# Moving the value copies and the second logits group at the head of a window-attention step

## The chip, the cores and the metric

One core of a Trainium2 chip runs the whole kernel. The metric is device time in microseconds (us) of one execution, lower is better.

## The reference

A Swin block on an input of 32 images of 56 x 56 tokens with 128 channels: layer norm, a cyclic shift by 3, windows of 7 x 7 tokens, attention with 16 heads of 8 channels with a relative position bias and a mask for the shifted edge windows, projection, residual; then layer norm, an MLP 128 to 512 to 128 with GELU, residual.

```python
y = _ln(x, norm1_g, norm1_b)
y = jnp.roll(y, (-SS, -SS), axis=(1, 2))
yw = y.reshape(B, nWh, WS, nWw, WS, C).transpose(0, 1, 3, 2, 4, 5).reshape(B * nW, N, C)
qkv = yw @ qkv_w.T + qkv_b
...
attn = jnp.einsum('bhqd,bhkd->bhqk', q * scale, k)
...
attn = jax.nn.softmax(attn.reshape(B * nW, HEADS, N, N), axis=-1)
o = jnp.einsum('bhqk,bhkd->bhqd', attn, v)
...
o = o @ proj_w.T + proj_b
...
x = shortcut + o
h = _ln(x, norm2_g, norm2_b)
h = jax.nn.gelu(h @ fc1_w.T + fc1_b, approximate=False)
h = h @ fc2_w.T + fc2_b
return x + h
```

## The kernel before

The work is cut into 128 steps: 8 bands of 7 rows by 16 pairs of images. A step holds two images side by side (partitions 0 to 48 and 64 to 112 of most tiles) and 8 windows of each. The steps run as a software pipeline written out by hand: body `t` of each engine holds, in a fixed order, pieces of step `t+3` (load and statistics) down to step `t-3` (store). Each engine runs its own program in order, and waits on counting semaphores; nothing reorders at run time. So the order of the calls in each body is the order on the engine.

What matters here is the head of a body and its window loop, `for w in range(NW)` with `NW = 8`. A turn of that loop handles one window of both images (the change's title calls it a pair):

- TensorE (PE) makes the values of step `t` (line 910, 24 matmuls): windows 0 to 3 into PSUM bank 7 (`s_v` counts one), windows 4 to 7 into bank 6 (`s_v` counts two). Then it projects the attention output of step `t-1` (line 919, 14 matmuls in two signalled halves, 4 and 3 rows). Then comes the loop: `logits(t, w)` (lines 780 and 785, into banks 2 to 5, two window buffers), `pv(t, u)` (line 800, probabilities times values, into bank 6) in the even turns from 2, `fc2` of step `t-2` (lines 832 and 837, into bank 7) in the odd turns, and `max_logits(t+1, w)` (line 750, into banks 0 and 1), the logits of the next step, of which only the row maxima are needed.
- `max_logits(t+1, 0)` waits until the operands `mx_k` and `mx_q` are in (`s_mx_dma`; SyncE, whose queue is SPq, issues them at lines 273 and 277), and until VectorE (DVE) has read the projection out of banks 0 and 1 (`s_x1`, line 682). `max_logits(t+1, w)` for a later `w` waits for the row maxima of `w-1` (`s_max`).
- VectorE casts the hidden layer (`hid_high`, line 580), copies one quarter of the values (line 673, image 0 of bank 7) to `v_own`, adds projection and residual (`x1`, line 682, two halves), and then, in the loop, takes the row maxima (`row_maxima`, line 587) with pieces of layer norm statistics (line 506) in between.
- ScalarE (ACT) does two GELUs (line 421), loads the table of exp (`load_table`, line 397: a table load and a one-element activation), copies two quarters of the values (line 483, image 1 of both banks), then `exp` of window 0 (line 406), the last quarter of the values (line 488, image 0 of bank 6), and the other `exp`s, with copies of `pv` (line 414).
- GpSimd (POOL) makes `hid_lo` (line 375) from the GELU output, which the last matmuls of `fc2` (line 837) need.

`v_place(im, b)` is the place of one image and one bank in `v_own`, `v_made(im, b)` the PSUM it is copied from (bank `7 - b`). `logits(t, w)` waits for `exp` of `w-2` where it reuses a buffer, and `pv(t, 0)` for `exp` of windows 0 and 1 and for all value copies. `fc2(t-2, 1, ...)` in turn 1 writes bank 7, and so waits until the values in it have been copied.

Of the kernel before, what the change touches and what calls it, by code (L numbers as in the profile page):

```python
# [9 lines left out]
ACT = mybir.ActivationFunctionType  # L10
# [39 lines left out]
def swin_block_kernel(nc, x, wqT, wkT, wvT, wvpT, wpT, w1T, w2T, cols, rows, table_k, table_q, ident, eye,  # L50
# [11 lines left out]
    with ctx:  # L62
# [324 lines left out]
        @block.scalar  # L387
        def _(act):
            act.wait_ge(s_w, 16 * N_W)

            nc.scalar.mul(w_q, w_q, HD ** -0.5).then_inc(s_inita, 1)
            nc.scalar.mul(col[:, BQ:BQ + 1], col[:, BQ:BQ + 1], HD ** -0.5).then_inc(s_inita, 1)
            act.wait_ge(s_inita, 2)

            def load_table(function):

                nc.scalar.activation(scrap[:, :], col[0:1, 0:1], function)

            def exp_pair(n, w):
                if w >= 4 or past(n, 0):  # L400
                    act.wait_ge(s_pv, NU * n + w // 2 - 1)
                act.wait_ge(s_st, NW * n + w + 1)
                if w < CH and exists(n - 2):
                    act.wait_ge(s_hid_lo, CH * (n - 2) + w + 1)
                b = 2 + 2 * (w % 2)
                nc.scalar.activation(probs[0:KP, w % 4, :].rearrange("p (b c) -> p b c", b=2),  # L406
                                     ps[0:KP, b:b + 2, 0:HB * WT], ACT.Exp).then_inc(s_exp, 1)

            def copy_pv(n, u):
                act.wait_ge(s_pv, NU * n + u + 1)  # L410
                if u == 0 and past(n, 0):
                    act.wait_ge(s_o_dma, N_O * n)
                    act.wait_ge(s_sum_dma, N_SUM * n)
                nc.scalar.activation(pv_sb[:, :, 2 * u * WT:2 * (u + 1) * WT],  # L414
                                     ps[:, 6, 0:NG * 2 * WT].rearrange("p (g q) -> p g q", g=NG),
                                     ACT.Copy).then_inc(s_pv_sb, 1)

            def gelu(n, c):
                act.wait_ge(s_fc1, CH * n + c + 1)
                bank = 2 + 2 * (c % 2)  # L420
                nc.scalar.activation(hid[:, c, :].rearrange("p (b q) -> p b q", b=2), ps[:, bank:bank + 2, 0:HT],  # L421
                                     ACT.Gelu, bias=col[:, BF + c:BF + c + 1], scale=1 / W_SCALE).then_inc(s_gelu, 1)

            def body(t, edge, odd):
                if exists(t - 1):
                    copy_pv(t - 1, NU - 1)
                n = t - 2
                if exists(n):
                    act.wait_ge(s_t2, n + 1)
                    if past(n, 0):  # L430
                        act.wait_ge(s_fc1, CH * n)
                    nc.scalar.activation(h_hi[:, :].rearrange("p (i c) -> p i c", c=TP),
                                         tokens_of(2)[:, 0:WS, 0:TP], ACT.Copy).then_inc(s_h_hi, 1)
                n = t + 1
                if exists(n):

                    act.wait_ge(s_t1, n + 1)
                    if past(n, 1):
                        act.wait_ge(s_v, 2 * (n - 1))
                    else:  # L440
                        act.wait_ge(s_initp, 1)
                    src = tokens_of(0)[:, 0:WS, 0:TP].rearrange("p i (m c) -> p i m c", m=2)
                    dst = yT_hi[odd(1)][:, :, :, 0:WT].rearrange("p w m (i j) -> p w m i j", i=WS)
                    last_w = NW - 1
                    kept = WS - SS
                    def put(o, a):
                        return nc.scalar.activation(o, a, ACT.Copy)
                    for im in range(2):
                        put(dst[:, 0:last_w, im, :, :].rearrange("p w i j -> p i w j"),
                            src[:, :, im, SS:SS + last_w * WS].rearrange("p i (w j) -> p i w j", j=WS))  # L450
                    put(dst[:, last_w, :, :, 0:kept].rearrange("p m i j -> p i m j"),
                        src[:, :, :, W - kept:W])
                    put(dst[:, last_w, :, :, kept:WS].rearrange("p m i j -> p i m j"),
                        src[:, :, :, 0:SS]).then_inc(s_y_hi, 1)
                if exists(t - 2):
                    load_table(ACT.Gelu)
                    gelu(t - 2, 0)
                    gelu(t - 2, 1)
                n = t + 1
                if exists(n):  # L460

                    if past(n, 0):
                        act.wait_ge(s_mx_dma, N_MX * n)
                        act.wait_ge(s_st_dma, N_ST * n)
                    for j, (hi, bank, b) in enumerate(((k_hi, 0, BK), (q_hi, 6, BQ))):
                        act.wait_ge(s_qk, 2 * n + j + 1)
                        nc.scalar.activation(hi[:, :, :, :].rearrange("p w m q -> p m w q"),
                                             ps[:, bank:bank + 2, 0:BT].rearrange("p m (w q) -> p m w q", w=NW),
                                             ACT.Identity, bias=col[:, b:b + 1]).then_inc(s_hi, 1)
                if exists(t - 2):  # L470
                    gelu(t - 2, 2)
                    gelu(t - 2, 3)
                if exists(t):
                    load_table(ACT.Exp)
                n = t
                if exists(n):
                    if past(n, 0):
                        act.wait_ge(s_pv, NU * n)
                    else:
                        act.wait_ge(s_init, 2)  # L480
                    for b in range(2):
                        act.wait_ge(s_v, 2 * n + b + 1)
                        nc.scalar.activation(v_place(1, b), v_made(1, b), ACT.Copy).then_inc(s_vown_b, 1)
                if exists(t):
                    for w in range(NW):
                        exp_pair(t, w)
                        if w == 0:
                            nc.scalar.activation(v_place(0, 1), v_made(0, 1), ACT.Copy).then_inc(s_vown_b, 1)
                        if w % 2 == 0 and w > 0:
                            copy_pv(t, w // 2 - 1)  # L490

            turns(body)


        @block.vector
        def _(dve):
# [96 lines left out]
            def body(t, edge, odd):  # L593
# [70 lines left out]
                if exists(t - 2):  # L664
                    hid_high(t - 2, 2)
                    hid_high(t - 2, 3)
                n = t
                if exists(n):

                    if past(n, 0):  # L670
                        dve.wait_ge(s_pv, NU * n)
                    dve.wait_ge(s_v, 2 * n + 1)
                    nc.vector.tensor_copy(v_place(0, 0), v_made(0, 0)).then_inc(s_vown, 1)
                n = t - 1
                if exists(n):

# [8 lines left out]
                for w in range(NW):  # L685
                    if exists(t + 1):
                        row_maxima(t + 1, w)
                    n = t - 1
                    if exists(n):

                        if w in (0, 1):
                            stats(x1, st2, (2 * w, 2 * w + 2))
                        if w == 2:
                            stats(x1, st2, (4, WS)).then_inc(s_st2, 1)
                        if w == 3:
                            aggregate(n, st2, s_st2, mv2, s_ln2)
                    n = t + 3
                    if exists(n):

                        if w == 4:  # L700
                            dve.wait_ge(s_x, loads(n, edge(n)))
                            stats(x_in[odd(3)], st1, (0, 1))
                        if w == 5:
                            stats(x_in[odd(3)], st1, (1, 4))
                        if w == 6:
                            stats(x_in[odd(3)], st1, (4, WS)).then_inc(s_st1, 1)
# [8 lines left out]
        def _(pe):  # L715
# [102 lines left out]
            def fc2(n, p, i):  # L818
                first, end = FC2_PARTS[p]
                if i == first and p == 1:  # L820
                    pe.wait_ge(s_hid_hi, CH * (n + 1))
                    if exists(n + 2):
                        pe.wait_ge(s_vown, n + 3)
                        pe.wait_ge(s_vown_b, 3 * (n + 2) + 1)
                    elif n > 0:
                        pe.wait_ge(s_fin, 2 * n)
                if i == first and p == 0:
# [13 lines left out]
            def body(t, edge, odd):  # L841
# [78 lines left out]
                        last.then_inc(s_proj, 1)  # L920
                for w in range(NW):
                    if exists(t):
                        if w != 1:
                            logits(t, w, edge, odd(0))
                        if w == 0:
                            logits(t, 1, edge, odd(0))
                        if w % 2 == 0 and w > 0:
                            pv(t, w // 2 - 1)
                    if exists(t - 2) and w % 2:
# [67 lines left out]
```

## Time and profile before

| | |
|---|---|
| median of three runs | 3900.76 us (3899.22 to 3903.62) |
| the profiled execution | 3904.86 us, its span 3903.1 us |
| busy share of the span | PE 96%, DVE 79%, POOL 74%, ACT 71% |
| granted TensorE clock, mean | 0.993 of full speed |

The span runs from the first to the last instruction in the trace; what lies around it is 1.8 us. Times in the trace are from the start of the span. A matmul's record begins at its issue and ends with a modelled end, so records of neighbouring matmuls overlap.

### The profile page before, as it was taken

The numbers are of one execution on the slowest core, as the hardware profiler recorded it, in microseconds if no ns is written. First come the engines' busy times: TensorE is split into PE (matmuls) and PEld (weight loads), VectorE is DVE, ScalarE is ACT, GpSimd is POOL, SyncE is SP. The second block draws the span as 40 slices with busy tenths as digits, with TensorE's granted clock in tenths as the row PEclk, the third lists the DMA queues.
The fourth block names the chain that finished last, engine by engine and source line by source line (L and its number), as shares of the span: only waits on it lengthen the run. The fifth ranks groups of instructions, "written<-read, shape, count | busy, mean of one in ns | idle before, by whom it ended". The sixth has DMA issues, their size and how long they took to land. (4 is left out here: it accounts for less than half of the span.)

```text
span 3903.1 us, 176619 instructions
## 1 busy us (share of the span) xinstructions
PE 3744.1 (96%) x75664; PEld 2946.8 (76%) x75664; DVE 3087.1 (79%) x7840; ACT 2776.0 (71%) x3840; POOL 2884.4 (74%) x3988
## 2 busy tenths in 40 slices
PE   2899999999999999999999999999999999999997
PEld 1677777777777777777777777777777777777776
DVE  6788878878878878878887888888888788888874
ACT  1677777777777777777777777777777777777774
POOL 5577777777777777777777777777777777777775
PEclk8999999999999999999999999999999999999999
DMA  2343334434434434433433344333344334333331
GB/s 76 106 119 118 115 112 118 119 111 116 121 114 115 118 115 118 117 115 115 118 117 111 115 119 116 114 117 116 111 118 120 112 116 119 115 115 117 117 108 58
DMA packets 603457, 441.97 MB, mean 113 GB/s; under 512 B 135939, under 2 KB 602227, under 8 KB 602675
## 3 DMA queue, kind: packets, MB, share of 16 engines
q1 hardware_dynamic: 602211, 428.86, 37.2%
q8 instruction: 597, 9.78, 1.1%
q14 instruction: 185, 1.52, 0.1%
q0 software_dynamic: 464, 1.81, 0.1%
HBM read 106.14 MB, written 51.46 MB: 40 GB/s over the span
## 5 line engine op out<-in xcount | busy, mean ns | idle before, releaser
L587 DVE TENSOR_REDUCE neg_max<-ps 113x16 f32<-113x784 f32 x1024 | 999.6, 976 | 545.5 <-PE ps L750 439.1
L406 ACT ACTIVATE probs<-ps 113x784 f32<-113x784 f32 x1024 | 848.1, 828 | 656.9 <-PE ps L785 539.5
L375 POOL TENSOR_TENSOR hid_lo<-probs,hid_hi 128x784 f16<-128x784 f32 x512 | 881.3, 1743 | 76.6 <-DVE hid_hi L580 76.3
L785 PE MATMUL ps<-st_q,st_k 128*49 128x196 f16 x8192 | 694.5, 249 | 0.0
L780 PE MATMUL ps<-bias,eye_k 106*64 106x392 f16 x4096 | 684.3, 331 | 0.0
L750 PE MATMUL ps<-mx_k,mx_q 128*49 128x196 f16 x8192 | 541.6, 253 | 60.3 <-DVE neg_max L587 52.4
L785 PEld LDWEIGHTS ps<-st_q,st_k 128*49 128x49 f16 x8192 | 440.2, 105 | 125.4 <-issue 0.5
L421 ACT ACTIVATE probs<-ps,col 128x784 f32<-128x784 f32 x512 | 467.6, 913 | 89.5 <-PE ps L814 60.1
L832 PE MATMUL ps<-w_hi,hid_hi 128*112 128x128 f16 x3584 | 521.7, 226 | 3.8 <-DVE hid_hi L580 3.0
L832 PE MATMUL ps<-w_lo,hid_hi 128*112 128x128 f16 x3584 | 498.8, 220 | 0.0
L832 PEld LDWEIGHTS ps<-w_hi,hid_hi 128*112 128x112 f16 x3584 | 417.7, 130 | 83.8 <-issue 79.4
L800 PE MATMUL ps<-probs,v_own 113*32 113x49 f32 x32768 | 470.3, 209 | 8.3 <-issue 7.6
L800 PEld LDWEIGHTS ps<-probs,v_own 113*32 113x32 f32 x32768 | 397.1, 110 | 92.3 <-issue 90.9
L750 PEld LDWEIGHTS ps<-mx_k,mx_q 128*49 128x49 f16 x8192 | 317.3, 103 | 137.6 <-DVE neg_max L587 74.4
L832 PEld LDWEIGHTS ps<-w_lo,hid_hi 128*112 128x112 f16 x3584 | 419.1, 131 | 0.0
L338 POOL TENSOR_SCALAR x_in<-x_in,rs,nm 112x128 f32<-112x128 f32 x896 | 389.4, 450 | 13.5 <-POOL nm L333 0.4
L338 POOL TENSOR_SCALAR z<-x,rs,nm 112x128 f32<-112x128 f32 x896 | 388.7, 450 | 13.5 <-POOL nm L333 0.4
L329 POOL TENSOR_TENSOR rs<-ve,half 112x7 f32<-112x7 f32 x256 | 380.4, 1486 | 21.3
L414 ACT ACTIVATE pv_sb<-ps 128x392 f32<-128x392 f32 x512 | 255.2, 498 | 182.0 <-PE ps L800 171.4
L356 POOL TENSOR_SCALAR r_hi<-sums 128x98 f16<-128x98 f32 x128 | 36.4, 284 | 461.3 <-DVE sums L628 461.3
L350 POOL TENSOR_TENSOR x_res<-x_res,proj_b 112x896 f32<-112x896 f32 x128 | 268.9, 2101 | 131.2 <-DMA x_res<-in_x 131.1
L837 PE MATMUL ps<-w_hi,hid_lo 128*112 128x128 f16 x3584 | 349.3, 220 | 3.4 <-POOL hid_lo L375 3.4
(119 smaller groups left out, 8009.9 us busy)
## 6 DMA issues: line engine op xcount, KB each, us to landing
st_k<-k_hi SPq DMA_DIRECT2D x256, 196.0 KB
st_q<-q_hi SPq DMA_DIRECT2D x1024, 49.0 KB
oT_raw<-pv_sb SPq DMA_DIRECT2D x256, 196.0 KB, 3.8
x_in<-in_x SPq DMA_DIRECT2D x224, 196.0 KB
x_res<-in_x SPq DMA_DIRECT2D x224, 196.0 KB
out_y<-y_out SPq DMA_DIRECT2D x224, 196.0 KB
mx_k<-k_hi SPq DMA_DIRECT2D x512, 49.0 KB
mx_q<-q_hi SPq DMA_DIRECT2D x128, 196.0 KB
```

Source lines behind the costliest of these rows:

```text
L329: nc.gpsimd.tensor_tensor(rs[:, :], ve[:, :], half[:, :], ALU.pow).then_inc(s_rs, 1)
L338: last = nc.gpsimd.tensor_scalar(z[:, i, :], src[:, i, :], rs[:, i:i + 1], nm[:, i:i + 1], ALU.mult, ALU.add)
L375: nc.gpsimd.tensor_tensor(hid_lo[:, c, :], hid[:, c, :], hid_hi[:, c, :], ALU.subtract).then_inc(s_hid_lo, 1)
L406: nc.scalar.activation(probs[0:KP, w % 4, :].rearrange("p (b c) -> p b c", b=2), ps[0:KP, b:b + 2, 0:HB * WT], ACT.Exp).then_inc(s_exp, 1)
L421: nc.scalar.activation(hid[:, c, :].rearrange("p (b q) -> p b q", b=2), ps[:, bank:bank + 2, 0:HT], ACT.Gelu, bias=col[:, BF + c:BF + c + ...
L587: nc.vector.tensor_reduce(neg_max[0:KP, :, :, w].rearrange("p e g -> p g e"), ps[0:KP, 0:2, :].rearrange("p b (g c) -> p (b g) c", g=2)[:, ...
L750: last = mm(group(im, 0, g, 256), mx_q[edge(n)][:, g, span], mx_k[:, g, :, span], start=True, stop=True)
L780: mm(ps[HP * im:HP * (im + 1), bank + b, 0:HB * WT], eye_k[0:BIAS_ROWS, kind, im, :], bias[0:BIAS_ROWS, b, :], start=True, stop=False)
L785: last = mm(group(im, bank, g, EQ * WT), st_k[par][:, g, span], st_q[par][:, :, g, span], start=False, stop=(g % 2 == 1))
L800: last = mm(ps[32 * r:32 * r + VC, 6, first:first + WT], v_own[0:KP, w, h, :], probs[0:KP, w % 4, h * WT:(h + 1) * WT], start=True, stop=True)
L832: mm(row, hid_hi[:, c, i * TP:(i + 1) * TP], w_part[:, c, :], start=(c == 0 and w_part is w2_hi), stop=False)
L837: last = mm(row, hid_lo[:, c, i * TP:(i + 1) * TP], w2_hi[:, c, :], start=False, stop=(c == CH - 1))
```

## The change

Three edits. ScalarE copies both images of bank 7 as soon as the values of windows 0 to 3 are there, ahead of its table load, and image 0 of bank 6 after the first `exp`, as before. VectorE no longer copies image 0 of bank 7 ahead of `x1`; it copies image 1 of bank 6 after the row maxima of turn 0. On TensorE the logits of window 1 come in turn 1, behind `max_logits(t+1, 0)`, and no longer ahead of it; the wait of `fc2` for bank 7 is changed to match.

```diff
@@ ScalarE body @@
-                if exists(t):
-                    load_table(ACT.Exp)
                 n = t
                 if exists(n):
                     if past(n, 0):
                         act.wait_ge(s_pv, NU * n)
                     else:
                         act.wait_ge(s_init, 2)
-                    for b in range(2):
-                        act.wait_ge(s_v, 2 * n + b + 1)
-                        nc.scalar.activation(v_place(1, b), v_made(1, b), ACT.Copy).then_inc(s_vown_b, 1)
+                    act.wait_ge(s_v, 2 * n + 1)
+                    for im in range(2):
+                        nc.scalar.activation(v_place(im, 0), v_made(im, 0), ACT.Copy).then_inc(s_vown_b, 1)
+                    load_table(ACT.Exp)
                 if exists(t):
                     for w in range(NW):
                         exp_pair(t, w)
                         if w == 0:
+                            act.wait_ge(s_v, 2 * t + 2)
                             nc.scalar.activation(v_place(0, 1), v_made(0, 1), ACT.Copy).then_inc(s_vown_b, 1)
@@ VectorE body @@
-                n = t
-                if exists(n):
-
-                    if past(n, 0):
-                        dve.wait_ge(s_pv, NU * n)
-                    dve.wait_ge(s_v, 2 * n + 1)
-                    nc.vector.tensor_copy(v_place(0, 0), v_made(0, 0)).then_inc(s_vown, 1)
@@
                     if exists(t + 1):
                         row_maxima(t + 1, w)
+                    if w == 0 and exists(t):
+                        if past(t, 0):
+                            dve.wait_ge(s_pv, NU * t)
+                        dve.wait_ge(s_v, 2 * t + 2)
+                        nc.vector.tensor_copy(v_place(1, 1), v_made(1, 1)).then_inc(s_vown, 1)
@@ TensorE fc2 @@
                     if exists(n + 2):
-                        pe.wait_ge(s_vown, n + 3)
-                        pe.wait_ge(s_vown_b, 3 * (n + 2) + 1)
+                        pe.wait_ge(s_vown_b, 3 * (n + 2) + 2)
@@ TensorE body @@
                     if exists(t):
-                        if w != 1:
-                            logits(t, w, edge, odd(0))
-                        if w == 0:
-                            logits(t, 1, edge, odd(0))
+                        logits(t, w, edge, odd(0))
```

## Rows read from the trace of the kernel before

**Rows 1.** The page's busy times; then one step's length, busy times and granted clock.

```profile
PE 3744.1 (96%) x75664; PEld 2946.8 (76%) x75664; DVE 3087.1 (79%) x7840; ACT 2776.0 (71%) x3840; POOL 2884.4 (74%) x3988
...
1948.37:1977.62 29.25, 28.92 (x595) 22.85 (x592) 23.66 (x62) 21.70 (x31) 21.55 (x31) 1.00 0.41 117
```

**Rows 2.** Waits of TensorE: engine line waited for: us, times, longest.

```profile
PE ps L750 <- DVE neg_max L587: 52.4, 140, 1.1
...
PE ps L750 <- DMA mx_q<-q_hi: 4.4, 1, 4.4
```

**Rows 3.** TensorE's timeline, head of one step: start, us, what [idle before].

```profile
1947.60 0.22 PE L910 MATMUL ps<-wv_lo,yT_hi 128*128 128x128 f16 x1
...
1948.36 1.78 PE L919 MATMUL ps<-w_p,oT 128*112 128x128 f32 x14
1950.07 0.36 PE L780 MATMUL ps<-bias,eye_k 106*64 106x392 f16 x2
...
1950.78 0.33 PE L780 MATMUL ps<-bias,eye_k 106*64 106x392 f16 x2
...
1951.46 0.51 PE L750 MATMUL ps<-mx_k,mx_q 128*49 128x196 f16 x8
1951.90 0.26 PE L832 MATMUL ps<-w_hi,hid_hi 128*112 128x128 f16 x1
...
1953.11 0.53 PE L750 MATMUL ps<-mx_k,mx_q 128*49 128x196 f16 x8 [0.33 <-DVE neg_max L587]
1953.47 0.33 PE L780 MATMUL ps<-bias,eye_k 106*64 106x392 f16 x2
...
1954.25 0.90 PE L800 MATMUL ps<-probs,v_own 113*32 113x49 f32 x64
1955.08 0.53 PE L750 MATMUL ps<-mx_k,mx_q 128*49 128x196 f16 x8
...
1956.22 0.26 PE L832 MATMUL ps<-w_hi,hid_hi 128*112 128x128 f16 x1
...
1957.03 0.44 PE L750 MATMUL ps<-mx_k,mx_q 128*49 128x196 f16 x6
```

**Rows 4.** VectorE's timeline over the same head.

```profile
1948.22 1.04 DVE L580 CAST hid_hi<-probs 128x784 f16<-128x784 f32 x2
1949.17 1.08 DVE L673 COPY v_own<-ps 49x512 f32<-49x512 f32 x1
1950.09 1.14 DVE L682 TENSOR_TENSOR x<-ps,x_res 112x512 f32<-112x512 f32 x2
1952.07 0.98 DVE L587 TENSOR_REDUCE neg_max<-ps 113x16 f32<-113x784 f32 x1 [0.85 <-DVE x L682]
1952.97 0.47 DVE L506 BATCH_NORM_STATS2 st<-x 112x6 f32<-112x128 f32 x2
1953.68 0.98 DVE L587 TENSOR_REDUCE neg_max<-ps 113x16 f32<-113x784 f32 x1 [0.24 <-PE ps L750]
```

**Rows 5.** Second half of x1, from the groups by shape: busy us, mean ns.

```profile
L682 DVE TENSOR_TENSOR x<-ps,x_res 112x384 f32<-112x384 f32 x128 | 68.6, 536 | 0.5 <-PE ps L919 0.5
```

**Rows 6.** GpSimd's timeline over the same head.

```profile
1948.86 3.57 POOL L375 TENSOR_TENSOR hid_lo<-probs,hid_hi 128x784 f16<-128x784 f32 x2 [0.56 <-DVE hid_hi L580]
```

**Rows 7.** ScalarE's timeline over the same head.

```profile
1945.66 1.91 ACT L421 ACTIVATE probs<-ps,col 128x784 f32<-128x784 f32 x2
1947.58 1.28 ACT L397 ACT_TABLE_LOAD   x1
1948.88 0.20 ACT L397 ACTIVATE scrap<-col 1x1 f32<-1x1 f32 x1
1949.09 2.08 ACT L483 ACTIVATE v_own<-ps 49x512 f32<-49x512 f32 x2
1951.19 0.82 ACT L406 ACTIVATE probs<-ps 113x784 f32<-113x784 f32 x1
1951.91 1.06 ACT L488 ACTIVATE v_own<-ps 49x512 f32<-49x512 f32 x1
1952.78 0.85 ACT L406 ACTIVATE probs<-ps 113x784 f32<-113x784 f32 x1
```

**Rows 8.** SyncE's queue, head of the same step, then of the step at 947 us.

```profile
1947.80 0.60 SPq L277 DMA_DIRECT2D mx_q<-q_hi  x1
1948.45 1.12 SPq L186 DMA_DIRECT2D out_y<-y_out  x2
...
946.63 0.60 SPq L277 DMA_DIRECT2D mx_q<-q_hi  x1
947.27 2.08 SPq L186 DMA_DIRECT2D out_y<-y_out  x2
```

**Rows 9.** DMA issues: KB each, median us from issue to landing.

```profile
oT_raw<-pv_sb SPq DMA_DIRECT2D x256, 196.0 KB, 3.8
...
r_rows<-r_lo SPq DMA_DIRECT2D x128, 24.5 KB, 2.4
```

## The prediction

> **What bounds the kernel now.** I read the busy shares first: TensorE is busy 96% of the span and no other engine over 79% [rows 1]. In a middle step it is busy 28.92 of 29.25 us at a granted clock of 1.00 [rows 1], which is its upper level, 2.4 GHz. So only what removes an idle stretch of TensorE, or adds one, can move the time. The view of waits says which idle stretch recurs in every step: line 750, the row-maximum logits, waits for VectorE's row maxima, 52.4 us in 140 waits, about one a step of 128 [rows 2]. TensorE's timeline gives the place: the second `max_logits` of the loop, at 1953.11, after 0.33 us idle [rows 3]. An `fc2` block followed by `max_logits` without a wait takes 1957.03 - 1956.22 = 0.81 us, here it takes 1953.11 - 1951.90 = 1.21, so the stall is **0.40 us** [rows 3]. Its cause is a chain: x1 ends at 1950.09 + 1.14 = 1951.23 [rows 4]; `max_logits` 0 is issued at 1951.46, when the logits of window 1 are out of the way [rows 3]; its row maxima run 1952.07 to 1953.05 [rows 4], and TensorE goes on 0.06 later. I take 0.06 us for every signal below. All working is for this step; the other steps without DMA trouble should look alike.
>
> **The change, part by part.** The times are what each event would become.
>
> *VectorE's copy leaves the way of x1.* It costs 1.08 us there [rows 4]. x1 then waits for TensorE: the first half needs 8 of the 14 projection matmuls, which are issued 1950.07 - 1948.36 over 14 = 0.12 us apart, so it can start at about 1949.55, after the cast (1949.26). The second half needs all 14, which end at 1948.36 + 1.78 = 1950.14 [rows 3], and takes 0.54 [rows 5]. x1 ends at 1950.20 + 0.54 = 1950.74, which is 0.49 earlier.
>
> *`max_logits` 0 ahead of logits 1.* Logits 0 are out at 1950.78 [rows 3], x1's signal comes at 1950.80, so `max_logits` 0 starts at **1950.80**, 0.66 earlier. The row maxima of window 0 follow at the same distance: 1951.41 to 1952.39. TensorE meanwhile: `max_logits` takes 1953.47 - 1953.11 = 0.36, logits with the change to `fc2` or `pv` 1954.25 - 1953.47 = 0.78 [rows 3]. So `fc2` starts at 1951.94 (now 1951.90), and `max_logits` 1 at 1952.75, 0.36 earlier. The maxima (1952.45 with the signal) no longer hold it. Nothing was added to TensorE: 0.36 is almost the whole stall. `fc2`'s last matmuls need `hid_lo`, which GpSimd ends at 1948.86 + 3.57 = 1952.43 [rows 6]; the last of the 12 is issued about 0.7 after the first, at 1952.6. It is covered, by 0.1 us. The new condition of `fc2` for bank 7 is covered by far (below, 1949.97). Unheld, TensorE would go on to logits 2 at 1953.11, `pv` 0 at 1953.89 and `max_logits` 2 at 1953.89 + 0.83 = 1954.72.
>
> *ScalarE.* Its wait for the values moves ahead of the table load. Bank 7 is written when 12 of 24 matmuls are through: 1947.60 + 0.22 = 1947.82 [rows 3]. The GELUs end at 1947.57 [rows 7], so ScalarE idles 0.3 us, which it did not before; queued behind are the table load and all `exp`s. Copies: 1947.88, and 2.08 for two to 1949.96. The table load with its one-element activation takes 1949.09 - 1947.58 = 1.51 [rows 7], so `exp` 0 starts at **1951.48** instead of 1951.19. From the start of `exp` 0 to the end of `exp` 1, with the copy in between, 1953.63 - 1951.19 = 2.44 [rows 7]: `exp` 1 ends at 1953.92, and `pv` 0 can start at **1953.98**. That holds TensorE by 0.09 us. Against 1954.25 the gain left is **0.27 us**.
>
> *VectorE's copy, now inside the loop.* Row maxima 0 end at 1952.39; copy (1.08), two statistics (0.47) and row maxima 1 (0.98) follow, each starting 0.09 before the one ahead ends, as now [rows 4]: 1952.39 + 1.08 + 0.47 + 0.98 - 0.27 = 1954.65, signal at 1954.71. `max_logits` 2 would be issued at 1953.98 + 0.83 = 1954.81, now 1955.08. So it is hidden, with 0.1 us to spare, and the step still keeps 0.27. `pv` 0 needs this copy at 1953.98; it ends at 1953.38. From there the loop has slack: the 140 waits on line 587 are about one a step [rows 2], so the later turns do not hold TensorE.
>
> *The table load beside the Trainium skill.* At this place the row shows 1.28 us of load begun 0.01 after the GELU's end, and the next activation 0.02 behind the load [rows 7]: no drain is to be seen. The Trainium skill (ScalarE: Activation LUTs, What ACT_TABLE_LOAD costs) gives 1283 ns for the load, which agrees, and a drain of about 1380 ns on each switch, which these rows do not show; by it, `pv` 0 would come 1.4 us later and the step would be slower by 1.1, a rival below.
>
> *The operands' transfer.* `max_logits` 0 is now wanted 0.66 earlier, and `mx_q` is the last of its five transfers, issued at 1947.80 [rows 8]. No row has its landing. Bounds: 2.4 us, a small transfer of the same queue, gives 1950.2; from above, TensorE had to wait for it only once in the kernel's 128 steps [rows 2], so it lands by about 1951.4, 3.6 us after issue (`oT_raw`, of its size, takes 3.8 [rows 9]). The first costs nothing; the second holds `max_logits` 0, and with it logits 1, `exp` 1 and the maxima, by 0.6 us, and takes all of the gain. I take the low end for most steps, since 2.4 is also the latency of the nearest single transfer, and a wait of 0.2 us for one step in five: the queue is sometimes slow (the same two issues of `out_y` behind it took 2.08 us instead of 1.12 [rows 8]). That is 0.04 us a step.
>
> *The rest.* What lies behind the loop, the chains of the sums and of `r_rows` to the next head among them, starts from the last `pv` of the step and moves with it. Semaphore conditions and the order of the first and last steps cost or give nothing that can be seen.
>
> **Sum.** 0.27 - 0.04 = 0.23 us a step; some 126 steps have both neighbours: 29 us. Against the profiled execution 3904.86 - 29 = 3876; the median of the runs is 4 us lower, 3900.76 - 29 = **3872 us**.
>
> **Rivals.**
> 1. *The exp chain does not hold.* If ScalarE's chain is 0.1 shorter than worked out, TensorE keeps 0.36: 126 x 0.36 = 45 us, 3856. For it: the margins are of 0.1 us. Against it: every term is a row. Chance 0.1.
> 2. *A transfer takes the stall's place.* `mx_q` lands near the upper bound in most steps; the stall moves from row maxima to the DMA and the time stays at 3895 to 3902. For it: `oT_raw`'s 3.8 us [rows 9]. Against it: those go two at a time, `mx_q` alone. Chance 0.08; a half-way case (0.1 to 0.15 left, 3882 to 3890) 0.12.
> 3. *The loop's copy binds VectorE.* Were the copy or the statistics 0.4 us longer in turn 0, `max_logits` 2 would wait as long as `max_logits` 1 did: 3898. Against it: the same shape took 1.08 in its old place. Chance 0.03.
> 4. *Slower: the table load behind the copies.* The load now lies on the chain from the values to `exp` 1 and `pv` 0. The chain decides from 0.27 us more than I worked out. If the switch cost twice there what it costs now, the 1.28 of a second load [rows 7], `pv` 0 comes at 1955.26, 1.0 us later than now: 126 us, 4027. This is the size of what the Trainium skill (ScalarE: Activation LUTs, What ACT_TABLE_LOAD costs) would add as a drain. Against it: the load shows no gap on either side [rows 7], and it is the same load after a like activation. A smaller lengthening (0.1 beyond the bound) gives 3913. Chance 0.05.
>
> **How the numbers follow.** The forecast, 3862 to 3881, has 0.62, rival 1 has 0.10, rival 2 0.20 with its half-way case, rival 3 0.03, rival 4 0.05. The range runs from 3858, just short of rival 1's end, to 3890, the half-way case's end; outside are most of rivals 1 to 4 proper, under 0.2. A change of 0.2% (8 us) is about what a measurement can tell from none. Faster by more than that: forecast, rival 1, half-way, a little of the rest, 0.86; same 0.09; slower 0.05.
>
> **What would show each step.** In the profile after: x1 beginning about 0.3 after the cast and ending 0.6 after the last projection matmul; `max_logits` 0 some 2.4 us after the first projection matmul (now 3.1); the 52.4 us of line 750 on line 587 nearly gone; line 800 with a new wait of about 0.1 us a step for `exp`; `exp` 0 about 0.3 later against the projection. Line 750 waiting for `mx_q` in many steps would show rival 2, a gap at the table load rival 4, line 750 still on line 587 in turn 2 rival 3. The prediction is wrong if the pitch of the steps, 29.25 us in this one, does not fall by 0.2 to 0.3.

## The result, and the profile after

The changed kernel takes 3918.31 us (median of 4 runs, 3915.66 to 3925.03), the kernel before 3901.45 beside it: ratio 1.0047, 95% interval 1.0034 to 1.0060. It is slower, by 17 us; the prediction was 3872. The profiled execution has a span of 3916.8 us at a mean granted clock of 0.994.

With the same work and nearly the same clock, TensorE is busy 27 us more than before and VectorE 49 us more (3744.1 and 3087.1 [rows 1]); how the waits of TensorE changed tells more. The page's first part, then the view of waits (engine, line, waited for: us in total, times, longest), TensorE's matmuls (PE) first and then its weight loads (PEld), which wait ahead of the matmuls. Lines 748 and 798 are lines 750 and 800 of the kernel before.

```profile
PE 3770.8 (96%) x75664; PEld 2948.0 (75%) x75664; DVE 3135.8 (80%) x7840; ACT 2800.4 (71%) x3840; POOL 2894.2 (74%) x3988
...
PE ps L748 <- DVE neg_max L587: 15.0, 31, 1.1
...
PEld ps L748 <- DVE neg_max L587: 48.8, 139, 1.4
PEld ps L798 <- ACT probs L406: 40.2, 122, 0.6
...
PEld ps L748 <- issue: 20.3, 103, 0.6
PEld ps L748 <- DMA mx_q<-q_hi: 12.0, 24, 5.0
```

The matmuls' own wait for row maxima fell from 52.4 to 15.0 us [rows 2], and this could be read as the forecast gain. It is not: the weight loads still wait for them once a step (139 times), if for less time than in the kernel before:

```profile
PEld ps L750 <- DVE neg_max L587: 74.4, 140, 1.4
```

They also wait once a step for `exp` (122 times, against 4 before). A wait can stand at the weight load and not at the matmul behind it, so one must read both rows.

TensorE's timeline gives the places, in a step whose projection begins at 1869.92 (before: 1948.36):

```profile
1869.92 1.78 PE L916 MATMUL ps<-w_p,oT 128*112 128x128 f32 x14
...
1872.49 0.53 PE L748 MATMUL ps<-mx_k,mx_q 128*49 128x196 f16 x8
1872.83 0.35 PE L778 MATMUL ps<-bias,eye_k 106*64 106x392 f16 x2
...
1874.44 0.53 PE L748 MATMUL ps<-mx_k,mx_q 128*49 128x196 f16 x8
...
1875.77 0.90 PE L798 MATMUL ps<-probs,v_own 113*32 113x49 f32 x64
1876.79 0.53 PE L748 MATMUL ps<-mx_k,mx_q 128*49 128x196 f16 x8
```

Counted from the start of the projection, as all times are from here on:

| issued at | before [rows 3] | worked out | after |
|---|---|---|---|
| `max_logits` 0 | 3.10 | 2.44 | 2.57 |
| `max_logits` 1 | 4.75 | 4.39 | 4.52 |
| `pv` 0 | 5.89 | 5.62 | 5.85 |
| `max_logits` 2 | 6.72 | 6.45 | 6.87 |

The step is ahead at `max_logits` 1, hardly so at `pv` 0, and behind at `max_logits` 2. `pv` 0 takes 0.83 us in the kernel before (5.89 to 6.72), and here 1.02 pass. The rest is `max_logits` 2 waiting for VectorE. Its timeline, in the same step:

```profile
1869.79 1.04 DVE L580 CAST hid_hi<-probs 128x784 f16<-128x784 f32 x2
1871.19 1.16 DVE L675 TENSOR_TENSOR x<-ps,x_res 112x512 f32<-112x512 f32 x2 [0.36 <-PE ps L916]
1873.11 0.98 DVE L587 TENSOR_REDUCE neg_max<-ps 113x16 f32<-113x784 f32 x1 [0.77 <-DVE x L675]
1874.12 1.10 DVE L685 COPY v_own<-ps 49x512 f32<-49x512 f32 x1
1875.26 0.49 DVE L506 BATCH_NORM_STATS2 st<-x 112x6 f32<-112x128 f32 x2
1875.76 0.97 DVE L587 TENSOR_REDUCE neg_max<-ps 113x16 f32<-113x784 f32 x1
```

From row maxima 0 to the end of row maxima 1, VectorE works through its queue with gaps of 0.01 to 0.04 us: 3.62 us (1873.11 to 1876.73), end at 6.81, `max_logits` 2 at 6.87. Before it was 2.59 with a pause of 0.24 [rows 4]. ScalarE, same step:

```profile
1869.49 2.25 ACT L481 ACTIVATE v_own<-ps 49x512 f32<-49x512 f32 x2 [0.35 <-PE ps L907]
1871.75 1.28 ACT L397 ACT_TABLE_LOAD   x1
1873.05 0.20 ACT L397 ACTIVATE scrap<-col 1x1 f32<-1x1 f32 x1
1873.26 0.82 ACT L406 ACTIVATE probs<-ps 113x784 f32<-113x784 f32 x1
1873.98 1.08 ACT L488 ACTIVATE v_own<-ps 49x512 f32<-49x512 f32 x1
1874.86 0.86 ACT L406 ACTIVATE probs<-ps 113x784 f32<-113x784 f32 x1
```

The two copies take 2.25 us instead of 2.08 [rows 7]; `exp` 0 starts at 3.34, `exp` 1 ends at 5.80.

Over 118 steps of the two traces, the mean issue of `max_logits` 2 went from 6.78 to 6.91, and the mean step from 29.51 to 29.64: 0.13 us in some 126 steps is 16 us, nearly the whole difference of 17.

### The profile page after: what moved, and what is told of

Its sections match the earlier page's. It is cut to its first block, busy times and chain, and to the rows that moved or that the text cites. A ratio compares the mean times of both kernels' runs of the same rounds, so it can differ in the third digit from the quotient of the medians.

```text
span 3916.8 us, 176619 instructions
## 1 busy us (share of the span) xinstructions
PE 3770.8 (96%) x75664; PEld 2948.0 (75%) x75664; DVE 3135.8 (80%) x7840; ACT 2800.4 (71%) x3840; POOL 2894.2 (74%) x3988
## 4 chain that ended last, share of the span: by engine, by line
PE 40%; DVE 5%; issue 3%; DMA 1%; POOL 1%; SPq 1%; ACT 0%; POOLq 0%; DVEq 0%; ACTq 0%
PE ps L812 6%; PE ps L829 5%; PE ps L748 5%; PE ps L798 5%; PE ps L778 4%; PE ps L783 3%; PE ps L879 3%; PE ps L916 3%; PE ps L834 2%; PE ps L907 2%; DVE v_own L685 2%; DVE neg_max L587 2%; PE ps L850 1%; PE ps L858 1%; DMA r_rows<-r_lo 1%
## 5 line engine op out<-in xcount | busy, mean ns | idle before, releaser
L783 PEld LDWEIGHTS ps<-st_q,st_k 128*49 128x49 f16 x8192 | 448.4, 105 | 121.1 <-issue 0.3
```

What stands on the lines that cost most here:

```text
L783: last = mm(group(im, bank, g, EQ * WT), st_k[par][:, g, span], st_q[par][:, :, g, span], start=False, stop=(g % 2 == 1))
```

## The experiments

The theory, called A in the expectations: VectorE's queue in turn 0 of the loop (row maxima 0, the copy, two statistics, row maxima 1) has become the bound of each step; behind it, ScalarE's chain (copies, table load, `exp` 0, copy, `exp` 1) holds `pv` 0 by less. Turn 0 is the first turn of the loop. The first rival is that the order of TensorE does the harm (B in the expectations), others that the order alone would bring the gain and the copies spoil it (C), that the copy harms in another way, or the table load. Names in the diffs are as in the change.

**Each half alone.** `order_only` is the kernel before with the change of TensorE's order and nothing else:

```diff
-                        if w != 1:
-                            logits(t, w, edge, odd(0))
-                        if w == 0:
-                            logits(t, 1, edge, odd(0))
+                        logits(t, w, edge, odd(0))
```

> Theory A (VectorE's turn 0 binds, and every part of the change needs the others): x1 still ends 2.87 us after the first projection matmul, so max_logits 0 can be issued at about 3.0 instead of 3.11, but logits 1 (0.68) now lie behind it: max_logits 1 at 4.95 instead of 4.75, slower by 0.2 us a step, about 3926. Rival B (the new order of TensorE is what costs the 17 us, the copies are neutral): 3918. Rival C (the order alone brings the gain that was forecast, the copies spoil it): 3870 to 3890.

3924.24 us beside 3900.2, ratio 1.0060 (1.0043 to 1.0077). `copies_only` is the changed kernel with these four lines put back:

```diff
-                        logits(t, w, edge, odd(0))
+                        if w != 1:
+                            logits(t, w, edge, odd(0))
+                        if w == 0:
+                            logits(t, 1, edge, odd(0))
```

> Theory A: max_logits 0 stays at 3.11 us after the projection begins, row maxima 0 end at 4.70, the copy, the two statistics and row maxima 1 follow end to end (1.11, 0.49, 0.98 and gaps of 0.03) and end at 7.34, so max_logits 2 comes at 7.40 instead of 6.72: 0.68 us a step, about 3987. Rival B: 3901, no change. Rival C: the copies alone cost about what the gain would have been, 3930 to 3950.

3966.85 us, ratio 1.0175 (1.0160 to 1.0190). Each half alone is slower than the kernel before, the copies by far more than the whole change (1.0047), the order by about as much. That puts out B, which had 3901 for `copies_only`, and C, which had a gain for `order_only`. With the order alone, TensorE waits for x1 ahead of `max_logits` 0; with the copies alone, for row maxima 1 as well as 0. The waits of matmuls, `order_only` and then `copies_only`:

```profile
PE ps L750 <- DVE x L682: 59.4, 124, 1.3
```

```profile
PE ps L748 <- DVE neg_max L587: 117.3, 256, 1.1
```

In `order_only`, `max_logits` 0, 1 and 2 come at 3.02, 4.97 and 6.94 (medians of 118 steps), worked out beforehand as 3.0 and 4.95. In `copies_only`, `max_logits` 2 comes at 7.39 as worked out (7.40), but the time is 20 us under the expected: its mean step is 0.49 us longer than before while `max_logits` 2 is 0.61 later in the mean, so 0.12 is regained in the rest of the step, which the expectation did not allow for; where it is regained was not looked into.

**Without the copy in the loop.** `no_loop_copy` leaves out the copy of image 1 of bank 6, so those values are missing from its output, and `pv`'s wait for it:

```diff
-                    if w == 0 and exists(t):
-                        if past(t, 0):
-                            dve.wait_ge(s_pv, NU * t)
-                        dve.wait_ge(s_v, 2 * t + 2)
-                        nc.vector.tensor_copy(v_place(1, 1), v_made(1, 1)).then_inc(s_vown, 1)
...
-                    pe.wait_ge(s_vown, n + 1)
```

> The changed kernel without VectorE's copy in the loop (image 1 of bank 6 is not copied, so those values are missing from the output). Theory A: row maxima 1 are ready when max_logits 1 is, and only ScalarE's chain to pv 0 is left: max_logits 2 at 6.67 us after the projection begins, against 6.87 changed and 6.72 before: about 25 us under the changed kernel, 3894. Rival (the copy is not what holds the step): 3915 to 3920. If ScalarE's chain does not hold either: 3875.

3889.48 us, ratio 0.9972 (0.9961 to 0.9983), 29 us under the changed kernel. Without the copy in the loop the kernel is no longer slower than the one before. Is it the copy itself or the length of the queue it joins? `stats_later` keeps it and takes something else out of turn 0:

```diff
-                        if w in (0, 1):
-                            stats(x1, st2, (2 * w, 2 * w + 2))
+                        if w == 1:
+                            stats(x1, st2, (0, 4))
```

> The changed kernel with the two statistics of turn 0 done in turn 1. Theory A: row maxima 1 start right behind the copy, at 5.34 us, and end at 6.32, under pv 0; as without the copy, ScalarE's chain alone holds: 3894. Rival (the copy itself, not the length of VectorE's queue, does the harm, by a port or a bank): 3910 to 3918. A second rival: the statistics in turn 1 delay row maxima 2: 3918 or more.

3893.9 us, ratio 0.9983 (0.9974 to 0.9993). It is the length: the copy is still there, and the harm is gone. `max_logits` 2 comes at 6.68 in both kernels, now 0.83 behind `pv` 0, which ScalarE holds at 5.84. One sees there the second, smaller bound.

**ScalarE's chain.** `table_first` puts the table load back ahead of the copies:

```diff
+                    load_table(ACT.Exp)
                     act.wait_ge(s_v, 2 * n + 1)
                     for im in range(2):
                         nc.scalar.activation(v_place(im, 0), v_made(im, 0), ACT.Copy).then_inc(s_vown_b, 1)
-                    load_table(ACT.Exp)
```

> The changed kernel with ScalarE's table load back ahead of its copies. Theory A: exp 0 starts at 3.0 us after the projection begins instead of 3.34 and pv 0 is no longer held, but row maxima 1 still end at 6.82 and hold max_logits 2 at 6.87: no change, 3918. Rival (the table load behind the copies is what made the change slower): the gain appears, 3875 to 3885.

3916.17 us, ratio 1.0034 (1.0021 to 1.0047): as the changed kernel (1.0047), the intervals overlap. `exp` 0 starts at 2.88 instead of 3.34 and `pv` 0 at its unheld 5.66, for nothing, since `max_logits` 2 waits for VectorE at 6.86. `both` makes this edit and that of `stats_later` together:

> The changed kernel with both repairs: statistics of turn 0 in turn 1, table load ahead of the copies. Theory A: row maxima 1 end at 6.32 us, pv 0 starts at its unheld 5.66, max_logits 2 at 6.49 instead of 6.68 with the statistics alone: 0.19 us a step or 24 us under that kernel, 3870, faster than both kernels. Rival (something else, a transfer or GpSimd, holds the step at about its old length): 3890 to 3895.

3878.33 us, ratio 0.9935 (0.9923 to 0.9948), some 40 us under the changed kernel. It is 8 us over the expected, but half of that is not the kernel's: the kernel before took 3904.36 us beside this run and 3900.2 beside those from which the 3870 was worked out. Some 4 us are left, which is no more than the interval leaves open. A step of it on TensorE, projection at 2029.07:

```profile
2031.64 0.53 PE L748 MATMUL ps<-mx_k,mx_q 128*49 128x196 f16 x8
...
2033.59 0.53 PE L748 MATMUL ps<-mx_k,mx_q 128*49 128x196 f16 x8
...
2034.73 0.90 PE L798 MATMUL ps<-probs,v_own 113*32 113x49 f32 x64
2035.56 0.36 PE L748 MATMUL ps<-mx_k,mx_q 128*49 128x196 f16 x4
```

`pv` 0 at 5.66 and `max_logits` 2 at 6.49 are 0.23 ahead of the kernel before, the size of the forecast. In the mean over steps 0.225 is gained at `max_logits` 2, 0.16 is left at the transposes of `z2` behind the loop, and 0.17 at the end of the step. What holds TensorE behind the loop in some steps was not tried. The 0.055 us lost there would be 7 us in 126 steps, enough for what is missing.

**Overlap.** The copies in the changed kernel did not overlap what is next to them, as they did before. There VectorE's copy of image 0 began 0.09 us before the end of the cast ahead of it [rows 4]; here 0.03 us lies between the row maxima and the copy of image 1, in all 127 steps. Image 0 is on partitions 0 to 48, image 1 on 64 to 112, and the other instructions beside the copies begin at partition 0. The second theory is that an instruction overlaps the tail of the one ahead only if both start at the same partition. `images_swapped` exchanges the images of bank 6 between the engines:

```diff
-                            nc.scalar.activation(v_place(0, 1), v_made(0, 1), ACT.Copy).then_inc(s_vown_b, 1)
+                            nc.scalar.activation(v_place(1, 1), v_made(1, 1), ACT.Copy).then_inc(s_vown_b, 1)
...
-                        nc.vector.tensor_copy(v_place(1, 1), v_made(1, 1)).then_inc(s_vown, 1)
+                        nc.vector.tensor_copy(v_place(0, 1), v_made(0, 1)).then_inc(s_vown, 1)
```

> The changed kernel with the images of bank 6 exchanged: VectorE copies image 0 in the loop, ScalarE image 1 after exp 0. Theory on overlap: VectorE's copy starts 0.09 us before the end of row maxima 0 and the statistics 0.15 before the end of the copy, which gives VectorE about 0.25 us; ScalarE loses its two overlaps (0.1 and 0.2), exp 1 ends at 6.15 instead of 5.79, pv 0 starts at 6.2 and max_logits 2 at 7.05 instead of 6.87: slower than the changed kernel, about 3938. Rival (the lost overlap comes from the waits ahead of the instructions or from the bank): both engines as in the changed kernel, 3918.

3936.86 us, ratio 1.0082 (1.0069 to 1.0096). VectorE and ScalarE in one step, projection at 2055.35 (the last row of ScalarE merges `exp` 1 and `exp` 2):

```profile
2058.56 0.97 DVE L587 TENSOR_REDUCE neg_max<-ps 113x16 f32<-113x784 f32 x1 [0.77 <-DVE x L675]
2059.45 1.06 DVE L685 COPY v_own<-ps 49x512 f32<-49x512 f32 x1
2060.37 0.44 DVE L506 BATCH_NORM_STATS2 st<-x 112x6 f32<-112x128 f32 x2
2060.73 0.95 DVE L587 TENSOR_REDUCE neg_max<-ps 113x16 f32<-113x784 f32 x1
```

```profile
2058.70 0.82 ACT L406 ACTIVATE probs<-ps 113x784 f32<-113x784 f32 x1
2059.55 1.10 ACT L488 ACTIVATE v_own<-ps 49x512 f32<-49x512 f32 x1
2060.68 1.54 ACT L406 ACTIVATE probs<-ps 113x784 f32<-113x784 f32 x2
```

The same operations on the same engines, with the same waits and the same bank; only the partitions differ. VectorE's copy now starts 0.08 ahead of the end of the row maxima and the statistics 0.14 ahead of the copy's end; row maxima 1 end at 6.33 instead of 6.81. The row maxima behind the statistics changed too, which the theory as stated does not cover: both start at partition 0 in either kernel, yet they overlap by 0.08 here and had 0.01 between them in the changed kernel. Only the copy ahead of the statistics has another start. Like the row maxima it reads PSUM, and the statistics do not, so what counts may be the last instruction that used the same memory; no run tests that by itself. ScalarE has lost what VectorE won: 0.03 us between `exp` 0 and the copy instead of 0.10 of overlap, 0.03 behind the copy instead of 0.20. `exp` 1 ends at 6.13, `pv` 0 starts at 6.18 (medians of the steps), and TensorE waits 51.3 us in 115 steps for line 406:

```profile
PE ps L798 <- ACT probs L406: 51.3, 115, 0.8
```

`both_rev` is `both` with ScalarE's first two copies in the order image 1, image 0 (`for im in (1, 0)`):

> As the one with both repairs, ScalarE copying image 1 of bank 7 ahead of image 0. Theory on overlap (an instruction overlaps the tail of the one ahead only if both start at the same partition): the second copy follows without overlap, but exp 0, which starts at partition 0 like it, starts about 0.2 us before its end, at 2.75 instead of 3.0. The time stays, 3870, since pv 0 is not held by ScalarE. Rival (a copy never overlaps what follows when it comes second, whatever the partitions): exp 0 at 3.0.

3879.32 us, ratio 0.9938 (0.9924 to 0.9952), the same as `both`; the 3870 was too low for the same reasons. `exp` 0 starts at 2.76 instead of 2.88, 0.21 ahead of the end of the copy of image 0 (medians of the steps). In `both`, behind the copy of image 1, it starts 0.02 after the end.

With this, turn 0 can keep all its pieces. `overlap_only` has the exchange of `images_swapped`, the table load first and the order image 1, image 0; its statistics stay in turn 0. `all_three` moves them too.

> The changed kernel with its six pieces in the same turns, but partitions paired: table load first, then ScalarE copies image 1 and image 0 of bank 7, and image 1 of bank 6 after exp 0; VectorE copies image 0 of bank 6 in the loop, statistics left in turn 0. Theory on overlap: exp 0 starts at 2.76 us, exp 1 ends at 5.55, pv 0 is unheld at 5.66; row maxima 1 end at 6.32 as with the images exchanged; max_logits 2 at 6.49, as in the kernel with both repairs: 3878. Rival (VectorE's turn 0 is still too long, its margin is used up in steps with a late transfer): 3883 to 3890.

3877.6 us, ratio 0.9936 (0.9923 to 0.9948). VectorE in the step at 2026.22, where row maxima 1 end at 6.33, under `pv` 0:

```profile
2029.42 0.98 DVE L587 TENSOR_REDUCE neg_max<-ps 113x16 f32<-113x784 f32 x1 [0.77 <-DVE x L675]
2030.31 1.09 DVE L685 COPY v_own<-ps 49x512 f32<-49x512 f32 x1
2031.23 0.45 DVE L506 BATCH_NORM_STATS2 st<-x 112x6 f32<-112x128 f32 x2
2031.60 0.95 DVE L587 TENSOR_REDUCE neg_max<-ps 113x16 f32<-113x784 f32 x1
```

> The same with the statistics of turn 0 in turn 1 as well. In most steps TensorE is unheld already, so 3878 like the kernel with both repairs; at most 2 us less, from steps with a late transfer. Rival (shortening VectorE's turn 0 further still pays): under 3872.

3877.16 us, ratio 0.9936 (0.9924 to 0.9947). The two cannot be told apart: once VectorE no longer holds TensorE in turn 0, more slack on VectorE brings nothing. `both`, `both_rev`, `overlap_only` and `all_three` beat the kernel before by 0.6%.

## Why the prediction was wrong

- **What bounds the kernel:** right. The stall of 0.4 us ahead of `max_logits` 1 is gone: 2.57 to 4.52 is 1.95, what `max_logits`, logits and `fc2` take.
- **VectorE's copy out of the way of x1:** right in kind. x1 ends at 1871.19 + 1.16, which is 2.43 (worked out 2.38). The signal was mis-sized: `max_logits` 0 is issued 0.14 after x1's end, not 0.06. The 103 waits of its weight loads that the view puts to "issue" are about one a step and belong here.
- **The step that failed: VectorE's copy, now inside the loop.** It said that copy, statistics and row maxima 1 follow "each starting 0.09 before the one ahead ends, as now", that row maxima 1 end at 1954.65 (6.29 after the projection's start) and that this "is hidden, with 0.1 us to spare". They end at 6.81. The 0.52 are: 0.14 from the late start of row maxima 0 (x1 0.05 later, its signal 0.08 longer); 0.12, 0.13 and 0.10 from three gaps of 0.03, 0.04 and 0.01 in the place of overlaps of 0.09; and 0.04 from a longer copy and statistics (1.10 and 0.49), less 0.01 for the row maxima. The overlap of 0.09 was read from a copy of image 0 and put on a copy of image 1; with the image exchanged, all three overlaps are there and the sum comes out at 6.33. So the copy's start partition is the cause of all three gaps, also of the one behind the statistics, where neither of the two instructions changed. `no_loop_copy` and `stats_later`, each of which takes one piece out of the queue, and `table_first`, which frees `pv` 0 and gains nothing, show that this queue made the kernel slower than before.
- **ScalarE:** the chain and its place right, its size 0.2 short. Two copies were taken as 2.08, from two of the same image; of different images they take 2.25, and they begin 0.05 later. `pv` 0 came at 5.85 instead of 5.62. So a second term failed: without VectorE's queue, this alone would have left 0.04 of the 0.27 (6.72 to 6.68), and `no_loop_copy` was 11 us faster than the kernel before, not 29.
- **The table load:** its row held in its new place, 1.28 us with 0.02 behind it. Of the drain that the Trainium skill (ScalarE: Activation LUTs, What ACT_TABLE_LOAD costs) gives, this trace shows nothing. Rival 4 is out.
- **The transfer:** sized well. The weight loads of line 748 wait for `mx_q` 24 times, one step in five, for 12.0 us in all (before: 2 times, 5.8 us), of which 5.0 are the longest one; the forecast had 0.2 us in one step of five. Rival 2 is out.
- **The rivals:** rival 3 named the place and the bound, and had a chance of 0.03, with 0.4 us as the point from which it takes the gain. Row maxima 1 ended 0.52 later than worked out, and the time went past no change to the other side. Rival 3 had put the extra time in the copy or the statistics themselves; these were 0.04 longer, the rest lay between the instructions and ahead of them. The margin was 0.1 us on a sum of several terms, and the range did not hold the case that three overlaps fail together, as they did, for one cause.

## What to carry to other kernels

A piece moved from one engine's wait into another of its stretches costs nothing only if that stretch is not about to become the bound: add up the queue there instruction by instruction, and distrust a margin of 0.1 us that rests on overlaps measured elsewhere. When an engine serves two partition ranges in turn, put next to each other the instructions that start at the same partition, and look at what the other engine loses by it: the exchange in `images_swapped` helped VectorE and made the kernel slower. Two halves can each be slower alone (0.6% and 1.8% here), less so together (0.5%), and gain once the next bounds are taken away too (0.6% in `overlap_only`, which has two more edits), so judge such a change by its next bound, and read the waits of the weight loads too. When an expected time is worked out from an earlier run, compare ratios: the kernel before moved by 4 us between runs.

## What the runs showed of the hardware

At the head of the step, an instruction on VectorE or ScalarE overlapped the end of the one ahead only where both started at the same partition; beside the copies this held in every step of the changed kernel and of `images_swapped`. On VectorE: the copy starting at partition 0 begins 0.08 before the end of row maxima starting at 0, the one starting at 64 begins 0.03 after it; the statistics behind them 0.14 before and 0.04 after. On ScalarE: `exp` behind a copy at partition 0 begins 0.20 to 0.22 before its end, behind a copy at 64 0.02 to 0.03 after. The same start is not enough: row maxima 1 began 0.01 after the statistics in the changed kernel, and `exp` 0 0.01 after the one-element activation, all starting at partition 0. Each of the two reads PSUM, and the last instruction of its engine that had read PSUM was a copy at 64; with a copy at 0 in that place (`images_swapped`), row maxima 1 overlapped the statistics by 0.08. That the last use of the same memory decides fits all these rows, but was not tested. Two copies of about 1.1 us that both start at partition 64 took 2.08 together [rows 7], one starting at 0 and one at 64 took 2.25. The Trainium skill (ScalarE: Activation LUTs, What ACT_TABLE_LOAD costs) says that back-to-back ACTIVATEs overlap by about 93 ns; the trace agrees for a copy at the same start behind `exp` 0 (0.10), has twice as much for `exp` 1 behind that copy (0.20), and shows none where the start changes. Whether the start itself counts or the whole range of partitions was not tried.
